# The sinks attention written as a stage of its own: V stationary, P moving, shares of the sum by DRAM

## The reference

```python
NQ, NKV, HD, SW = (32, 8, 64, 64)          # QM = 4 query heads for each key head
proj = x @ W_qkv                            # x: layer-normed residual, B=4, L=512, D=256
q, k, v = jnp.split(proj, (NQ * HD, (NQ + NKV) * HD), axis=-1)
q, k = _apply_rope(q, ...), _apply_rope(k, ...)
attn = jnp.einsum('bqhmd,bkhd->bhmqk', q, k) * sm_scale
mask = (q_pos >= k_pos) & (q_pos < k_pos + SW)
attn = jnp.where(mask, -jnp.inf, attn)      # a band of 64 keys is left out, all others are kept
w = jax.nn.softmax(jnp.concatenate([attn, sink], axis=-1), axis=-1)[..., :-1]
out = jnp.einsum('bhmqk,bkhd->bqhmd', w, v).reshape(B, L, NQ * HD)
x = x + out @ W_out
```

## Time and profile before

| | us |
|---|---|
| median of 3 runs | 4833.33 (4824.67 to 4838.3) |
| the profiled execution | 4832.96, its span 4831.2 |
| PE busy over the span | 3839.2 (79%) |
| DVE, ACT, POOL busy | 2728.5, 2175.6, 1575.5 |
| mean granted TensorE clock | 0.869 of full |
| the fifth stage, first weight load issued to last add to the residual | 1993.2 to 3509.1, 1515.9 |

### The profile page before, as it was taken

The page is one execution under the profiler, slowest core; times in us unless marked ns, Lnnn a source line. Parts: engine busy times, 40 slices in busy tenths (PEclk is TensorE's granted clock), DMA queues, the critical chain, the costliest instruction groups (busy, mean ns, idle before and its releaser), DMA issues. The chain is left out here.

```text
span 4831.2 us, 85299 instructions
## 1 busy us (share of the span) xinstructions
PE 3839.2 (79%) x24186; PEld 3073.7 (64%) x24187; DVE 2728.5 (56%) x6679; ACT 2175.6 (45%) x5347; POOL 1575.5 (33%) x2593
## 2 busy tenths in 40 slices
PE   7799759188899487299989989989937399999554
PEld 3455547166777365178878878878825288888543
DVE  5799566444454655456456456456453375566362
ACT  3789314044555133166566556556502254444211
POOL 0499425521223145433133133133226200000055
PEclk9799869688999588599999999999957699999766
DMA  2111315400000335200000000000043400000424
GB/s 73 31 46 48 138 46 138 102 5 1 1 0 0 123 111 122 92 1 0 1 1 0 1 1 0 1 1 0 1 154 58 104 1 1 2 1 1 154 35 99
DMA packets 112289, 205.06 MB, mean 42 GB/s; under 512 B 24048, under 2 KB 85744, under 8 KB 110144
## 3 DMA queue, kind: packets, MB, share of 16 engines
q1 hardware_dynamic: 78224, 131.89, 8.1%
q0 software_dynamic: 33792, 69.83, 6.7%
HBM read 146.93 MB, written 54.53 MB: 42 GB/s over the span
## 5 line engine op out<-in xcount | busy, mean ns | idle before, releaser
L2065 DVE TENSOR_REDUCE sa_mx<-bank 128x1 f32<-128x512 f32 x512 | 352.8, 689 | 438.4 <-PE bank L1775 438.3
L1802 PE MATMUL bank<-sa_v,sa_pT 128*128 (+1 forms) x4096 | 550.3, 277 | 0.7
L1939 ACT ACTIVATE sa_p<-bank,sa_nm 128x512 f32<-128x512 f32 x512 | 351.6, 687 | 384.5 <-DVE sa_nm L2070 382.7
L1802 PEld LDWEIGHTS bank<-sa_v,sa_pT 128*128 128x128 f32 x4096 | 501.4, 193 | 4.2 <-issue 3.1
L239 PE MATMUL bank<-ident,ln_stage 128*128 128x128 f32 x256 | 77.1, 434 | 412.4 <-DVE ln_stage L215 408.5
L1255 POOL DMA_INDIRECT ex_xr<-scratch_rows,mo_token x288 | 286.3, 994 | 349.5 <-issue 310.6
L1502 POOL TENSOR_TENSOR sa_t<-sa_qraw,sa_cos 128x64 f32<-128x64 f32 x256 | 83.6, 327 | 959.1 <-ACT sa_qraw L1924 959.1
L597 POOL TENSOR_TENSOR sc_h<-sc_h,sc_c 128x512 f32<-128x512 f32 x256 | 327.0, 1290 | 200.3 <-DVE sc_h L634 192.3
L1771 PE MATMUL bank<-sa_kT,sa_qT 128*128 (+1 forms) x1024 | 367.2, 440 | 2.8 <-ACT sa_qT L1930 2.8
L1785 PE MATMUL bank<-ident,sa_p 128*128 128x128 f32 x2048 | 313.1, 276 | 53.5 <-ACT sa_qT L1930 51.6
L634 DVE TENSOR_TENSOR_SCAN sc_h<-sc_da,bank 128x512 f32<-128x512 f32 x256 | 311.1, 1220 | 40.1 <-ACT sc_da L577 25.3
(11 more groups left out here) (346 smaller groups left out, 10044.2 us busy)
## 6 DMA issues: line engine op xcount, KB each, us to landing
scratch_ys<-ex_yo SPq DMA_DIRECT2D x192, 128.0 KB
mo_w_gu<-in_w_gu SPq DMA_DIRECT2D x2, 9216.0 KB, 26.3
sc_c<-scratch_c SPq DMA_DIRECT2D x64, 256.0 KB, 3.1
mo_w_dn<-in_w_dn SPq DMA_DIRECT2D x2, 4608.0 KB, 47.9
mo_w_dn<-in_w_dn SPq DMA_DIRECT2D x2, 4096.0 KB, 33.6
scratch_rows<-ln_stage POOLq DMA_DIRECT2D x64, 128.0 KB, 5.3
ex_xr<-scratch_rows,mo_token POOLq DMA_INDIRECT x288
scratch_sum<-zeros SPq DMA_DIRECT2D x2, 2176.0 KB, 10.4
```

Of the source, the lines that this page charges most:

```text
L1802: last = pe.matmul(OB[qt % 2][:, hh * P:(hh + 1) * P], pT[u % 2][:, kb * P:(kb + 1) * P], v, start=(kb == 0), stop=(kb == nb - 1))
L1939: act.activation(pr[u % 4][:, 0:keys(qt)], SC[u % 2][:, 0:keys(qt)], ACT.Exp, bias=nm[:, col:col + 1], scale=a.scale, accum_out=rs[:, col: ...
L2065: dve.reduce_max(mx[:, col:col + 1], SC[u % 2][:, 0:keys(qt)], AX) \
```

## The change

The fifth stage gets a function of its own, `sinks`, in one block, with all loops written out instead of hardware loops; the other stages are as they were (some semaphores are shared under new names, and the eight PSUM banks are now cuts of one tensor).

- Two heads at a time: a step is a query tile and a pair of heads, 256 steps, two to a quad. Scores of a step go to two banks, and one DVE instruction takes the maximum of both.
- `values` is turned round. V is split into a high and a low fp32r part that lie side by side, 64 + 64 columns, and is the stationary operand; P transposed moves, 256 columns (two heads), also split in high and low. So a step has 8 products with 256 columns, and gives the output transposed, with the share of V's low part in partitions 64 to 127.
- For that both engines handle every transposed P: ACT copies each to the high part (`high_p`), DVE subtracts to get the low part (`low_p`). ACT copies the low half of the output (`low_y`), DVE adds the halves (`add_y`).
- The output is not scaled by DVE. `invert` gives 1/sum with queries in partitions; SP writes it to DRAM (512 elements of 4 bytes) and reads it back broadcast over partitions in two DMAs of 64 x 1 KB; POOL multiplies (`keep_y`) and writes the result in the transposed form that the last product needs. `turn_y` goes.
- K is kept in two versions, the second with high and low halves swapped (four more ACT copies for each key tile); Q no longer needs a swapped copy.
- The copy of the projected Q moves from ACT to DVE (`fetch_q`); adding the sink's share moves from DVE to POOL.
- The layer norm is applied batch by batch: 4 tiles before the first batch, 4 in each change of batch. The output product of a batch stands among the next batch's keys and values.

The diff, cut:

```diff
+def sinks(c):
...
+        def groups(steps):
+            for g in range(G):
+                steps(g, g == 0, g == G - 1)
...
+                    def steps(g, first, last):
+                        for qt in range(QUADS):
+                            q, u = (b * G + g) * QUADS + qt, qt % 2
+                            turn = (b * G + g) * (QUADS // 2) + (qt // 2 + 1)
+                            cold = first and b == 0 and qt < 2
+                            row = ROWS[qt:qt + 1, :]
+                            sp.wait_ge(*at("normed", q + 1))
+                            sp.dma_start(row.rearrange("o (h p) -> p (o h)", p=P),
+                                         rinv[:, u * HG:(u + 1) * HG], allow_slow_non_contiguous=True) \
+                              .then_inc(sig[f"rput{u}"].sem, 16)
+                            sp.wait_ge(*at(f"rput{u}", turn * 16))
+                            if not cold:
+                                sp.wait_ge(*at("ykept", q - 1))
+                            for half in range(2):
+                                sp.dma_start(share[u][half * D:(half + 1) * D, :],
+                                             row[:, half * 2 * P:(half + 1) * 2 * P].to_broadcast([D, 2 * P])) \
+                                  .then_inc(sig[f"share_in{u}"].sem, 16)
+                    groups(steps)
...
+                    def sink_minus_max(q, g, qt):
+                        cut = slice((qt % 2) * HG, (qt % 2 + 1) * HG)
+                        pool.wait_ge(*at("negged", q * 2 + 2))
+                        pool.tensor_tensor(es[:, cut], nm[:, cut], sink[:, bass.ds(g * HG, HG)], ALU.add) \
+                            .then_inc(*inc("sunk"))
+                    def total(q, qt):
+                        cut = slice((qt % 2) * HG, (qt % 2 + 1) * HG)
+                        pool.wait_ge(*at("sink_exped", q + 1))
+                        pool.tensor_tensor(rs[:, cut], rs[:, cut], es[:, cut], ALU.add).then_inc(*inc("own_n"))
+                    def keep_y(q, g, qt, before):
+                        u = qt % 2
+                        turn = (b * G + g) * (QUADS // 2) + (qt // 2 + 1 - before * (QUADS // 2))
+                        pool.wait_ge(*at("yadded", q * 2 + 2))
+                        pool.wait_ge(*at(f"share_in{u}", turn * 32))
+                        two = lambda x: x.rearrange("p (c n) -> p c n", c=2)
+                        spot = two(yT[:, bass.ds(g * (2 * SEQ) - before * (2 * SEQ), 2 * SEQ)])
+                        pool.tensor_tensor(spot[:, :, qt * P:(qt + 1) * P], two(yraw[u][:, :]), two(share[u][:, :]),
+                                           ALU.mult).then_inc(*inc("ykept"))
...
+                    def scores(g, p):
+                        N = (b * G + g) * STEPS_ + p
+                        q = (b * G + g) * QUADS + p // 2
+                        qt, s_ = divmod(p, 2)
+                        if not (isinstance(N, int) and N < 2):
+                            pe.wait_ge(*at("exped", N * 2 - 2))
+                        if s_ == 0:
+                            pe.wait_ge(*at("qkept", q + 1))
+                        lo, hi = max(qt * P - P, 0), (qt + 1) * P
+                        for h in range(2):
+                            bank, hh = SC[2 * s_ + h], 2 * s_ + h
+                            for w in range(2):
+                                pe.matmul(bank[:, :], qT[qt % 2][:, hh * P:(hh + 1) * P],
+                                          kT[w][:, bass.ds(g * SEQ, SEQ)], start=(w == 0), stop=False)
+                            last = pe.matmul(bank[:, lo:hi], identb[:, :], mask[:, MW - (hi - lo):MW],
+                                             start=False, stop=True)
+                        last.then_inc(*inc("scored"))
...
+                    def turn_p(N, p):
+                        for h in range(2):
+                            pe.wait_ge(*at("exped", N * 2 + (h + 1)))
+                            if not (isinstance(N, int) and N == 0):
+                                pe.wait_ge(*at("kept_d", N * 2 + (h - 1)))
+                            for kb in range(TPB):
+                                last = pe.transpose(PT[h][:, kb * P:(kb + 1) * P], pr[h][:, kb * P:(kb + 1) * P],
+                                                    c.ident[:, :])
+                            last.then_inc(*inc("turned"))
...
+                    def values(N, g, p, before):
+                        pe.wait_ge(*at("kept_d", N * 2 + 2))
+                        if not (isinstance(N, int) and N == 0):
+                            pe.wait_ge(*at("yadded", N))
+                        for kb in range(TPB):
+                            for w in range(2):
+                                last = pe.matmul(OB[:, 0:2 * P],
+                                                 vv[:, bass.ds(g * WR + (kb * KH * WR - before * WR), WR)],
+                                                 pT[p % 2][w][:, kb * 2 * P:(kb + 1) * 2 * P],
+                                                 start=(kb == 0 and w == 0), stop=(kb == TPB - 1 and w == 1))
+                        last.then_inc(*inc("summed"))
...
+                    def steps(g, first, last):
+                        I = b * G + g
+                        for p in range(STEPS_):
+                            N = I * STEPS_ + p
+                            qt, s_ = divmod(p, 2)
+                            q = I * QUADS + qt
+                            if s_ == 1 and (qt + 1 < QUADS or not last):
+                                turn_q(q + 1, qt + 2 < QUADS or not last)
+                            scores(g, p)
+                            if p >= 2:
+                                values(N - 2, g, p - 2, 0)
+                            elif not first:
+                                values(N - 2, g, p - 2 + STEPS_, 1)
+                            if s_ == 0 and (qt + 2 < QUADS or not last):
+                                project(q + 2, *((g, qt + 2) if qt + 2 < QUADS else (g + 1, qt + 2 - QUADS)))
+                            if p >= 1:
+                                turn_p(N - 1, p - 1)
...
+                    for i in range(TPB):
+                        keys_values(b, i)
+                        if i >= 1:
+                            turn_keys(b, i - 1)
+                        if i == 1:
+                            project(first_q, 0, 0)
+                        if b and i >= 1:
+                            if i == 1:
+                                pe.wait_ge(*at("yadded", b * G * STEPS_))
+                                pe.wait_ge(*at("wo_in", 16))
+                            product(b - 1, i - 1)
...
+                    def high_p(N, p):
+                        for h in range(2):
+                            act.wait_ge(*at("turned", N * 2 + (h + 1)))
+                            if h == 0 and not (isinstance(N, int) and N < 2):
+                                act.wait_ge(*at("summed", N - 1))
+                            act.activation(pT[p % 2][0][:, :].rearrange("p (k n) -> p k n", k=TPB)
+                                           [:, :, h * P:(h + 1) * P],
+                                           PT[h][:, :].rearrange("p (k n) -> p k n", k=TPB), ACT.Copy) \
+                               .then_inc(*inc("kept_a"))
...
+                    def maximum(N, g, p):
+                        qt, s_ = divmod(p, 2)
+                        col = (qt % 2) * HG + 2 * s_
+                        dve.wait_ge(*at("scored", N + 1))
+                        dve.reduce_max(mx[:, 2 * s_:2 * s_ + 2],
+                                       c.psum[:, 2 * s_ * 512:(2 * s_ + 2) * 512].rearrange("p (h n) -> p h n", h=2),
+                                       AX).then_inc(*inc("maxed"))
+                        dve.wait_ge(*at("maxed", N + 1))
+                        dve.scalar_tensor_tensor(out=nm[:, col:col + 2], in0=mx[:, 2 * s_:2 * s_ + 2], scalar=-SCALE,
+                                                 in1=negsink[:, bass.ds(g * HG + 2 * s_, 2)],
+                                                 op0=ALU.mult, op1=ALU.min).then_inc(*inc("negged"))
+                    def low_p(N, p):
+                        for h in range(2):
+                            dve.wait_ge(*at("kept_a", N * 2 + (h + 1)))
+                            spot = lambda w: pT[p % 2][w][:, :].rearrange("p (k n) -> p k n", k=TPB) \
+                                [:, :, h * P:(h + 1) * P]
+                            dve.tensor_tensor(spot(1), PT[h][:, :].rearrange("p (k n) -> p k n", k=TPB),
+                                              spot(0).bitcast(F32), ALU.subtract).then_inc(*inc("kept_d"))
+                    def add_y(N, q, p):
+                        qt, s_ = divmod(p, 2)
+                        dve.wait_ge(*at("ylow", N + 1))
+                        if s_ == 0 and not (isinstance(q, int) and q < 2):
+                            dve.wait_ge(*at("ykept", q - 1))
```

(12 more changed lines are left out.)

427 lines of the change are left out of this document (419 added, 8 removed).

## The result

| | before | after |
|---|---|---|
| median, us | 4831.57 (4 runs beside those of after) | 4982.77 (4963.45 to 4986.13, 4 runs) |
| ratio to before | 1 | 1.0305, 95% interval 1.0274 to 1.0335 |
| span of the profiled execution | 4831.2 | 4961.7 |

The account below looks back on a forecast made before the run. PE bounds the stage; afterwards the ACT and DVE chain sets a quad of 8.48 us instead of 9.49. Savings 129 + 32 + 6 + 10 = 177 us take 4833 to about 4655 us; range 4535 to 4770.

Parts of the forecast that it names:

- Shares by DRAM: Loop of write, read back and `keep_y`: transfers take 6.3 us, 8.3 allowed before anyone waits, so priced at nothing.
- slower: Same loop through DRAM makes the kernel slower than before once the transfers take 11.0 us; at 12 us 4894; chance 0.06.
- SP isn't full: SP's queue: it waits for its write before issuing the reads, but needs only 4 us of a quad's 8.48.
- The values: Values product on PE: 8 products a step at 0.133 us, 1.07 a step and 2.13 a quad, instead of 3.60.
- The hand-over: From `turn_p` through ACT's copy and DVE's subtractions to PE's values product: 2.77 us, PE waiting 0.73 or 0.38 a step.
- the 177 of the sum: Total saving in us: 129 from the quads, 32 from changes of batch, 6 from the last output, 10 from the start.
- the quad of 9.49: Upper bound of a quad, 9.49 us, said to be reached if each of the chain's five terms is half as long again.
- The change of batch: Between batches of the stage: 51 us instead of 61.7, three times, saving 32 us.
- The clock: Rival: PE's pauses bring the lower clock; a tenth of the quads at that level adds 80 us, 4735; chance 0.07.
- PE as the bound: Rival: cheaper hand-over or faster copies leave PE the bound, a quad about 7.6 us, 113 us less, 4542; chance 0.12.
- DVE held by POOL: Rival: DVE's bias is held by POOL, at worst 0.3 us a step, in about half the steps: 4695; chance 0.08.

Follow-up runs that it names:

- the run with 8-byte pieces: Against the changed kernel, each quad's shares are written as 256 pieces of 8 bytes and POOL reads them with a stride, nothing left out; 4598.63 us, ratio 0.9529.
- the run with the late `keep_y`: Against the changed kernel, POOL does `keep_y` behind `put_q`, the sink's subtraction and the total instead of ahead of them; 5001.15 us, ratio 1.0367.

## Why the prediction was wrong

**The step that failed is "Shares by DRAM"**, the one that I priced at nothing. Its sum was 3.0 + 0.5 + 2.6 + 0.2 = 6.3 us, with 8.3 allowed, so the wait was taken as covered. Measured: 9.47 from the write's issue to the reads' and 3.77 to POOL's start, 13.2 us. The 3.0 for the write came from a row of 128 KB in 2048 pieces, that is 64 bytes each: I matched the number of pieces and not their size and place, while the runs show that the number hardly matters (8.47 us for 512, 7.52 for 256). I had said that pieces of 4 bytes had no row, and then took the nearest row as the price instead of as one end of a range.

**The mechanism had been written down**, as the rival "slower", with the right turning point (11.0 us) and a chance of 0.06. Its own formula, given the measured 13.2, says (13.2 + 8.7) / 2 = 10.95 us a quad and 4655 + 128 x (10.95 - 8.48) = 4971 us; 4983 was measured. The inversions say the same: 369.7 / 128 = 2.89 us a quad more than the 8.05 of the run with 8-byte pieces, 10.94. The error is one term of 6 us that should have been wide. But the fit doesn't prove that it was this loop alone. SP's own cycle, 10.6 us, is nearly as long, and in the run with the late `keep_y`, where POOL's 3.75 us are out of the loop and the formula gives (13.2 + 8.7 - 3.75) / 2 = 9.1 at most, the quads got no shorter.

**"SP isn't full"** was wrong for the same reason: instead of 4 us in a quad of 8.48 it went round in 10.6. This is the bound that the late `keep_y` left in place, and no rival had priced it.

**Right, as the run with 8-byte pieces shows**, where the loop is out of the way. PE over one quad:

```profile
2458.64 1.22 PE L2449 MATMUL bank<-sa_pT,sa_v 128*128 128x256 f32 x8 [0.58 <-DVE sa_pT L2718]
2459.70 0.88 PE L2399 MATMUL bank<-sa_wq,sa_xb 128*128 128x256 f32 x6
2460.42 1.04 PE L2439 MATMUL bank<-ident,sa_p 128*128 128x128 f32 x8
...
2463.04 1.23 PE L2449 MATMUL bank<-sa_pT,sa_v 128*128 128x256 f32 x8
2464.10 1.04 PE L2439 MATMUL bank<-ident,sa_p 128*128 128x128 f32 x8
...
2466.87 1.22 PE L2449 MATMUL bank<-sa_pT,sa_v 128*128 128x256 f32 x8 [0.55 <-DVE sa_pT L2718]
```

- The values: 2458.64 to 2459.70, 1.06 us for 8 products, 0.133 each (forecast 1.07). Turning the product round does what it says.
- The hand-over: the path is as forecast, and the wait ends with DVE's subtraction. Its length was 2.77 us in the forecast. It is 2.77 in the second step here (2464.10 to 2466.87) by coincidence; in the first it is 2.62 (2460.42 to 2463.04), and 2.61 is the median of all steps. The rows of the other engines, first for the usual step and then for the long one:

```profile
2461.06 1.09 ACT L2585 ACTIVATE sa_pT<-bank 128x512 fp32r<-128x512 f32 x2 [0.78 <-PE bank L2439]
2461.69 1.29 DVE L2718 TENSOR_TENSOR sa_pT<-bank,sa_pT 128x512 fp32r<-128x512 f32 x2 [0.63 <-ACT sa_pT L2585]
...
2464.30 0.73 POOL L2250 TENSOR_TENSOR sa_qst<-sa_qrot,zeros 128x256 fp32r<-128x256 f32 x1
2464.32 0.72 DVE L2709 SCALAR_TENSOR_TENSOR sa_nm<-sa_mx,sa_negsink 128x2 f32<-128x2 f32 x1
...
2465.53 1.29 DVE L2718 TENSOR_TENSOR sa_pT<-bank,sa_pT 128x512 fp32r<-128x512 f32 x2
```

  Usually it is 0.64 + 0.63 + 1.29 + 0.06: PE starts 0.06 us after DVE ends (2462.98 to 2463.04), where 0.24 had been added. In the long step DVE's bias, 0.16 us in the median, took 0.72 beside POOL's 0.73, and the subtraction began 0.16 us later.
- Sizes off: two hand-overs of 2.61 instead of 2.77 and a projection of 0.72 instead of 0.80 make the quad 8.06 us, not 8.48; this one is 8.23, the median 8.05. 128 x 0.43 = 55 us more, with the 177 of the sum 232; measured 4825.4 - 4598.6 = 227.
- A bound that doesn't add up: the quad of 9.49 was said to be that of five terms half as long again. By the forecast's own sum that would be 8.48 + 2 x 1.39 = 11.25; 9.49 is reached when they are 18% longer.
- The change of batch: from the end of the last values product to the next scores it was

```profile
2309.14 1.22 PE L2449 MATMUL bank<-sa_pT,sa_v 128*128 128x256 f32 x8 [0.70 <-DVE sa_pT L2718]
...
2361.45 0.72 PE L2427 MATMUL bank<-sa_kT,sa_qT 128*128 128x512 f32 x2 [0.51 <-DVE residual L2685]
```

2361.45 - 2310.36 = 51.1 us, forecast 51; the other two took 51.6.

**The rivals.** The clock did fall to 0.92 in the changed kernel, but behind the stalls, and it was 1.00 without them. PE as the bound decided nothing: without the loop a quad is between PE's own 7.37 and the 9.49 of before. DVE held by POOL did happen, as in the long step above, but what that step lost by it was 0.16 us, and the quads came out shorter than forecast all the same.

## What to carry to other kernels

- A transfer that closes a loop between engines is priced by its completion, issue to release, and by how its far side is cut; where no row has the same size and distance of pieces, take a range from both ends and let the chances follow it.
- When a small tile is to be transposed by a DMA, keep at least two words together and let the engine that reads it use the stride: the write's wait fell from 8.47 to 2.74 us with 8-byte pieces, at no cost on POOL that a run could tell apart (`keep_y` 0.74 us, not 0.73).
- Issuing a slow write early doesn't hide it if what is urgent is issued behind it on the same queue.

## What the runs showed of the hardware

- 4-byte pieces that touch in DRAM: 8.47 us of waiting for 512, 7.52 for 256; at a distance of 8 bytes 3.16; touching pieces of 8 bytes 2.74, of 16 bytes 1.32. Whether it comes from two pieces in one 8-byte word or from 16 in 64 bytes wasn't told apart: all runs fit both. Why the chip is slow there is not shown; the time lies behind the last byte, with the DMA engines at a share of 0.00 for the last 5 us.
- The Trainium skill, page "DMA: Bandwidth & Descriptors", table of specifications, says that below 512 bytes a transfer does read-modify-write. No run here shows that step itself; all the pieces here, of 4 to 16 bytes, are below that size, and the waits went from 1.32 to 8.47 us.
- Reads whose bytes had moved by 2314 were reported at 2319.8, behind the completion of an earlier write on the same queue.
- After 6.5 us of idleness PE ran at a granted clock of 0.50 (1.20 us for two score products instead of 0.71).
